# The opening of an attention and expert kernel: x in two halves, layer norm on DVE, high weights on ACT, first jobs round four banks, V among the maxima

## The reference

```
x = x + ln(attention(ln(x)))     16 heads of width 16; q, k, v, out projections with bias; softmax over 1024 keys
x = x + ln(experts(ln(x)))       16 gated experts of hidden width 128, top 8 by sigmoid gate, plus one shared expert
```

## Time and profile before

| | us |
|---|---|
| median of 3 runs | 2800.32 (2798.92 to 2801.91) |
| the profiled execution | 2801.8 |
| its span, first to last instruction | 2799.9 |
| PE busy, DVE busy | 2667.4 (95%), 2203.5 (79%) |
| first instruction on x (DVE statistics) | 6.37 |
| first maxima tile on PE | 45.36 |
| first score tile on PE | 93.11 |

### The profile page before, as it was taken

The page is one execution under the profiler, slowest core; times in us unless marked ns, Lnnn a source line. Parts: engine busy times, 40 slices in busy tenths (PEclk is TensorE's granted clock), DMA queues, the critical chain, the costliest instruction groups (busy, mean ns, idle before and its releaser), DMA issues.

```text
span 2799.9 us, 49038 instructions
## 1 busy us (share of the span) xinstructions
PE 2667.4 (95%) x17634; PEld 1756.9 (63%) x17634; DVE 2203.5 (79%) x4585; ACT 1628.2 (58%) x3159; POOL 1042.5 (37%) x1057
## 2 busy tenths in 40 slices
PE   5999999999999999999998999999999999999997
PEld 3445444454454444544543488888888888888886
DVE  5798999999999999999999576666666666666654
ACT  1578878878878888788788733333333333333332
POOL 4042563644635626545457453111111111111112
PEclk8899999999999999999999999999999999999999
DMA  5102223223123232320232323223232232222222
GB/s 119 27 28 58 66 72 71 61 66 66 43 66 66 61 71 59 79 66 28 66 80 88 90 69 103 76 72 81 84 84 80 72 82 83 79 71 84 80 72 53
DMA packets 126595, 197.39 MB, mean 70 GB/s; under 512 B 12288, under 2 KB 74768, under 8 KB 124304
## 3 DMA queue, kind: packets, MB, share of 16 engines
q1 hardware_dynamic: 126352, 194.25, 26.7%
HBM read 108.74 MB, written 17.30 MB: 45 GB/s over the span
## 4 chain that ended last, share of the span: by engine, by line
PE 72%; DVE 23%; issue 2%; POOL 1%; ACT 1%; DMA 0%; POOLq 0%; SPq 0%; ACTq 0%; DVEq 0%
DVE score_max L1122 18%; PE y_bank L746 14%; PE g_bank L732 13%; PE u_bank L732 13%; PE o_bank L572 12%; PE sm_bank L562 9%; PE st_bank L549 6%; PE job_bank L664 2%; DVE qk_parts L1144 1%; DVE xT_lo L1140 1%; PE job_bank L687 1%; PE job_bank L700 0%; DVE row_max L1129 0%; POOL x_in L1494 0%; DVE stats L1081 0%
## 5 line engine op out<-in xcount | busy, mean ns | idle before, releaser
L1122 DVE TENSOR_REDUCE score_max<-sm_bank 128x1 f32<-128x512 f32 x2048 | 1278.7, 683 | 96.1 <-PE sm_bank L562 92.1
L1014 ACT ACTIVATE probs<-st_bank 128x512 f32<-128x512 f32 x2023 | 1077.3, 604 | 273.4 <-PE st_bank L549 264.2
L562 PE MATMUL sm_bank<-qk_stack 64*128 64x512 f32 x2048 | 814.7, 459 | 78.6 <-DVE score_max L1122 72.1
L549 PE MATMUL st_bank<-qk_stack 64*128 64x512 f32 x2023 | 744.5, 426 | 1.8 <-ACT probs L1014 1.5
L562 PEld LDWEIGHTS sm_bank<-qk_stack 64*128 64x128 f32 x2048 | 363.0, 187 | 443.4 <-DVE score_max L1122 416.4
L572 PE MATMUL o_bank<-probs,v_quad 128*32 128x512 f32 x4096 | 549.4, 609 | 0.7 <-ACT probs L1014 0.7
L549 PEld LDWEIGHTS st_bank<-qk_stack 64*128 64x128 f32 x2023 | 350.1, 185 | 230.5 <-ACT probs L1014 189.4
L1269 DVE TENSOR_TENSOR h<-gate_act,u_bank 128x512 f32<-128x512 f32 x256 | 176.3, 689 | 311.4 <-ACT gate_act L968 311.3
L968 ACT ACTIVATE gate_act<-g_bank 128x512 f32<-128x512 f32 x272 | 163.0, 599 | 417.2 <-PE u_bank L732 417.1
L979 ACT ACTIVATE h_hi<-h 128x512 fp32r<-128x512 f32 x272 | 172.5, 634 | 325.3 <-DVE h L1272 287.8
L1552 POOL TENSOR_SCALAR f_x_in<-f_x_in,f_mv,f_rstd 128x256 f32<-128x256 f32 x64 | 90.5, 1424 | 616.9 <-DVE f_rstd L1183 616.9
(11 more groups left out here) (216 smaller groups left out, 4354.4 us busy)
## 6 DMA issues: line engine op xcount, KB each, us to landing
cb<-comb_dram SPq DMA_DIRECT2D x256, 256.0 KB, 3.4
qk_stack<-qk_parts SPq DMA_DIRECT2D x180, 256.0 KB, 5.5
x_in<-in_x SPq DMA_DIRECT2D x8, 1024.0 KB, 5.4
o_part<-o_sb SPq DMA_DIRECT2D x64, 128.0 KB, 2.7
sum_part<-o_sb SPq DMA_DIRECT2D x64, 128.0 KB, 2.8
x_res<-in_x SPq DMA_DIRECT2D x16, 512.0 KB, 3.9
x<-x_res SPq DMA_DIRECT2D x16, 512.0 KB, 3.6
f_x_in<-x SPq DMA_DIRECT2D x16, 512.0 KB, 3.9
```

Of the source, the lines that this page charges most:

```text
L549: mm(bank_of(tile)[:, :], k_stack[q][p][rows, kc * CH:(kc + 1) * CH], q_stack[q][p][rows, f * HALF:(f + 1) * HALF], start=True, stop=True) ...
L562: mm(sm_bank[n % RING][:, :], q_stack[q][p][rows, tok:tok + CH], k_stack[q][p][rows, half * HALF:(half + 1) * HALF], start=True, stop=True ...
L1014: nc.scalar.activation(probs[kc % 2][:, HEAD_AT[j], :], bank_of(4 * U + j)[:, :], ACT.Exp).then_inc(exp_done, 1)
L1122: v.reduce_max(score_max[f][:, HC * (2 * p + e) + c, half:half + 1], sm_bank[n % RING][:, :], AX_X).then_inc(smax_read, 1)
```

## The change

Six edits, all in the opening:

- x of batch 0 is loaded in two halves, each with a semaphore of its own (`half_loaded`). `ident`, the biases and `out_bias` are issued on ACT's queue; the raw weights have a semaphore each.
- The layer norm of batch 0 is wholly on DVE: statistics by half, aggregates, twelve steps of the reciprocal square root (`first_rstd`), eight normalisations. POOL's order becomes: memsets of quads 0 and 1, low parts of wv and wo, memsets of quads 2 and 3.
- ACT makes the four high parts as the weights arrive (with the 1/4 for q in it); DVE makes the low parts of wq and wk after the norm, POOL those of wv and wo. ACT waits for all low parts before QK job 4.
- The first jobs go round four banks (`job_bank`, `o_bank`, `st_bank` 0 and 1).
- On SP the first loads of the stacks leave out the small copy (a semaphore increment stands for it), and `load_x(1)` with `load_shift(0, 0)` comes after all four stacks.
- The V jobs are issued in pairs of matmuls, one pair behind each of the last 24 maxima tiles of step 1 (`first_v`).

```diff
-        first_bank = [job_bank, o_bank]
+        first_bank = [job_bank, o_bank, st_bank[0], st_bank[1]]
...
         def _(sp):
-            sp.dma_start(x_in[:, :, :], xv[:, 0:CHUNKS, :]).then_inc(x_loaded, 16)
-            sp.dma_start(ident[:, :], ident_dram).then_inc(const_loaded, 16)
+            for i in range(2):
+                half = slice(i * HC, (i + 1) * HC)
+                sp.dma_start(x_in[:, half, :], xv[:, half, :]).then_inc(half_loaded[i], 16)
             for n, w in (("q", wq), ("k", wk), ("v", wv), ("o", wo)):
-                sp.dma_start(w_raw[n], w.rearrange("(k p) d -> p k d", p=128)).then_inc(const_loaded, 16)
-            sp.dma_start(bias_raw[:, :, :], biases).then_inc(const_loaded, 16)
-            for i in range(2):
-                sp.dma_start(out_bias[:, i, :], ob.partition_broadcast(128)).then_inc(const_loaded, 16)
+                sp.dma_start(w_raw[n], w.rearrange("(k p) d -> p k d", p=128)).then_inc(w_raw_loaded[n], 16)
...
                     sp.wait_ge(st_ready, 4 * (UNITS * (B - 1) + 16 * (q + 1)))
-
-                sp.dma_start(qk_stack[q][SHIFT_ROW:SHIFT_ROW + 65:64, :, 0, :].bitcast(F32),
-                             qk_stack[q][ZERO_ROW:ZERO_ROW + 65:64, :, 0, :].bitcast(F32)).then_inc(stack_loaded[q][0], 16)
+                if first:
+
+                    sp.sem_inc(stack_loaded[q][0], 16)
+                else:
+
+                    sp.dma_start(qk_stack[q][SHIFT_ROW:SHIFT_ROW + 65:64, :, 0, :].bitcast(F32),
+                                 qk_stack[q][ZERO_ROW:ZERO_ROW + 65:64, :, 0, :].bitcast(F32)).then_inc(stack_loaded[q][0], 16)
                 for p in range(2):
...
             for q in range(QUADS):
-                if q == QUADS - 1:
-                    load_x(1)
-                    load_shift(0, 0)
                 sp.wait_ge(stacks_set, 5 * (q + 1))
                 load_stack(0, q, True)
+            load_x(1)
+            load_shift(0, 0)
...
-            pe.wait_ge(const_loaded, 16 * 8)
+            pe.wait_ge(const_loaded, 16 * 3)
             for n, (kind, i) in enumerate(FIRST_JOBS):
                 if (kind, i) == ("QK", 0):
-                    pe.wait_ge(weights_split, 9)
-                job(kind, 0, i, job_bank=first_bank[n % 2], banks=2)
-            pe.wait_ge(job_read["QK"], nth("QK", 0, 7))
-            before.clear()
+                    pe.wait_ge(weights_hi, 2)
+                    pe.wait_ge(weights_lo["dve"], 2)
+                job(kind, 0, i, job_bank=first_bank[n % 4], banks=4)
+
+            def first_v(n):
+
+                i, t = n // 6, n % 6
+                if t == 0:
+                    if i == 0:
+                        pe.wait_ge(job_read["XT"], nth("XT", 0, 3))
+                        pe.wait_ge(weights_hi, 4)
+                        pe.wait_ge(weights_lo["pool"], 2)
+                    pe.wait_ge(*before.pop(0))
+                    before.append((job_read["V"], nth("V", 0, i)))
+                steps = [(k, a, w) for k in range(KD) for a, w in PARTS]
+                c, bank = 2 * i + t // 3, first_bank[(i + 1) % 4]
+                for z in (2 * (t % 3), 2 * (t % 3) + 1):
+                    k, a, w = steps[z]
+                    last = mm(bank[:, (c % 2) * D:(c % 2 + 1) * D], xT[a][:, k, c * CH:(c + 1) * CH],
+                              w_parts["v"][w][:, k, :], start=(z == 0), stop=(z == len(steps) - 1))
+                if t == 5:
+                    last.then_inc(job_ready["V"], 1)
+
             for S in range(2):
...
                     smax(S, S, n // 4, n % 4, False)
+                    if S == 1 and n >= CHUNKS:
+                        first_v(n - CHUNKS)
                 if S == 0:
-                    job("SH", 0, 0)
-            for i in range(4):
-                job("V", 0, i, job_bank=first_bank[(i + 1) % 2], banks=2)
-            before.pop(0)
+                    job("SH", 0, 0, job_bank=first_bank[0], banks=4)
+            pe.wait_ge(job_read["V"], nth("V", 0, 2))
+            del before[:-1]
             for tile in range(8):
...
-            act.wait_ge(weights_split, 9)
+            act.dma_start(ident[:, :], ident_dram).then_inc(const_loaded, 16)
+            act.dma_start(bias_raw[:, :, :], biases).then_inc(bias_loaded, 16)
+            for i in range(2):
+                act.dma_start(out_bias[:, i, :], ob.partition_broadcast(128)).then_inc(const_loaded, 16)
+            for n in "qkvo":
+                act.wait_ge(w_raw_loaded[n], 16)
+                nc.scalar.activation(w_parts[n][0][:, :, :], w_raw[n], ACT.Copy,
+                                     scale=DH ** -0.5 if n == "q" else 1.0).then_inc(weights_hi, 1)
             act.wait_ge(bias_set, 2)
             for n, (kind, i) in enumerate(FIRST_JOBS):
-                job(kind, 0, i, first_bank[n % 2])
+                if (kind, i) == ("QK", 4):
+
+                    act.wait_ge(weights_lo["dve"], 2)
+                    act.wait_ge(weights_lo["pool"], 2)
+                job(kind, 0, i, first_bank[n % 4])
             job("SH", 0, 0)
             for i in range(4):
-                job("V", 0, i, first_bank[(i + 1) % 2])
+                job("V", 0, i, first_bank[(i + 1) % 4])
...
+            def first_rstd():
+
+                dve.wait_ge(mean_x_ready, CHUNKS)
+                v.tensor_scalar(var_x[:, :], mv_x[:, :, 1], EPS, None, ALU.add).then_inc(first_chain, 1)
+                dve.wait_ge(first_chain, 1)
+                v.tensor_scalar(rstd_x[:, :].bitcast(I32), var_x[:, :].bitcast(I32), 1, None,
+                                ALU.logical_shift_right).then_inc(first_chain, 1)
+                dve.wait_ge(first_chain, 2)
+                v.tensor_scalar(rstd_x[:, :].bitcast(I32), rstd_x[:, :].bitcast(I32), -1, RSQRT_SEED, ALU.mult,
+                                ALU.add).then_inc(first_chain, 1)
+                for i in range(3):
+                    dve.wait_ge(first_chain, 3 * i + 3)
+                    v.scalar_tensor_tensor(newton[:, :], rstd_x[:, :], -0.5, rstd_x[:, :], ALU.mult, ALU.mult).then_inc(first_chain, 1)
+                    dve.wait_ge(first_chain, 3 * i + 4)
+                    v.tensor_tensor(newton[:, :], newton[:, :], var_x[:, :], ALU.mult).then_inc(first_chain, 1)
+                    dve.wait_ge(first_chain, 3 * i + 5)
+                    v.scalar_tensor_tensor(rstd_x[:, :], newton[:, :], 1.5, rstd_x[:, :], ALU.add, ALU.mult).then_inc(first_chain, 1)
+                dve.wait_ge(first_chain, 12)
+
+            def first_weight_lo(n, scale):
+                dve.wait_ge(weights_hi, "qkvo".index(n) + 1)
+                v.scalar_tensor_tensor(w_parts[n][1][:, :, :], w_raw[n], scale, w_parts[n][0][:, :, :].bitcast(F32),
+                                       ALU.mult, ALU.subtract).then_inc(weights_lo["dve"], 1)
+
             for c in range(CHUNKS):
-                ln_x_stats(0, c)
+                if c % HC == 0:
+                    dve.wait_ge(half_loaded[c // HC], 16)
+                v.bn_stats(stats[:, c, :], x_in[:, c, :]).then_inc(stats_x_done, 1)
             for c in range(CHUNKS):
                 ln_x_aggr(0, c)
-            seed_x(0)
-            dve.wait_ge(const_loaded, 16 * 8)
-            v.tensor_scalar(scaled[:, :, :], w_raw["q"], DH ** -0.5, None, ALU.mult).then_inc(weights_split, 1)
+            first_rstd()
+            for c in range(CHUNKS):
+                v.tensor_scalar(x_in[:, c, :], x_in[:, c, :], mv_x[:, c, 0:1], rstd_x[:, c:c + 1],
+                                ALU.subtract, ALU.mult).then_inc(x_normed, 1)
+            dve.wait_ge(bias_loaded, 16)
             v.tensor_scalar(bias[:, 0, :], bias_raw[:, 0, :], DH ** -0.5, None, ALU.mult).then_inc(bias_set, 1)
             v.tensor_copy(bias[:, 1:3, :], bias_raw[:, 1:3, :]).then_inc(bias_set, 1)
+            first_weight_lo("q", DH ** -0.5)
+            first_weight_lo("k", 1.0)
             dve.wait_ge(bias_set, 2)
-            dve.wait_ge(weights_split, 1)
-            raw = {"q": scaled[:, :, :], "k": w_raw["k"], "v": w_raw["v"], "o": w_raw["o"]}
-            for n in "qkvo":
-                v.tensor_copy(w_parts[n][0][:, :, :], raw[n]).then_inc(weights_split, 1)
-            for i, n in enumerate("qkvo"):
-                dve.wait_ge(weights_split, 2 + i)
-                v.tensor_tensor(w_parts[n][1][:, :, :], raw[n], w_parts[n][0][:, :, :].bitcast(F32),
-                                ALU.subtract).then_inc(weights_split, 1)
-
             for n, (kind, i) in enumerate(FIRST_JOBS):
-                job(kind, 0, i, first_bank[n % 2])
+                job(kind, 0, i, first_bank[n % 4])
             for S in range(2):
...
             wait_apart(pool, two_set, 1, passed["pool"])
-            set_stacks(0)
-            norm_x(0)
-            for q in range(1, QUADS):
+            def first_weight_lo(n):
+                wait_apart(pool, weights_hi, "qkvo".index(n) + 1, passed["pool"])
+                g.tensor_tensor(w_parts[n][1][:, :, :], w_raw[n], w_parts[n][0][:, :, :].bitcast(F32),
```

(22 more changed lines are left out.)

## The result

The changed kernel takes 2811.45 us (median of 7, 2808.45 to 2813.82) against 2800.32 for the kernel before (7, 2796.5 to 2801.91): ratio 1.0038, 95% interval 1.0029 to 1.0047. I had forecast 2780, faster. Its profiled execution took 2809.14, with a span of 2807.3, 7.4 above the span before.

The account below looks back on a forecast made before the run. The prediction took the opening's chain of waits before the first score (93.11 us) as what the edits shorten, the PE/DVE-bound loop staying unchanged. Gains of 13.2 and 7.0 make 20.2 us off 2800.3, forecast 2780; range 2775 to 2787.

Parts of the forecast that it names:

- term 2: From the first maximum to the first score, now 47.75 us: 8.3 saved by dropping the V burst, less 1.3, gains 7.0.
- 0.43 + 2 x 0.21 = 0.85 a slot: Step 1: PE time at 1.2 GHz for one maximum and two V matmuls of 256 columns, against DVE's 0.595 us.
- rival 1: Step 1: V among the maxima doesn't lift the clock; 24 slots lag 5.8 us instead of 1.3, 2784.5; chance 0.14.
- the rise of the clock after 5.5 us of dense PE: Step 1: V among the maxima makes PE dense, so the clock rises after 5.5 us; lag until then 1.3 us.
- term 1: The start of the first maximum moves from 45.36 to 32.2 us: gains 13.2, with ends of 8 and 16.
- normalising on DVE ... I take 0.27: Layer norm of batch 0: each of eight 128x256 normalisations takes 0.27 us on DVE, all ready at 13.1.
- Rival 2: Opening norm: DVE waits behind POOL's two low parts, two waits of 1.29 make 2.6 us, 2782.6; chance 0.13.
- QK jobs 0 to 3: Opening: from the first QK matmul to the end of DVE's fourth, 9.73 us becomes 9.4 with four banks.
- SP to the first maximum: Stack 0: from SP's release to the first maximum, 7.45 us minus 0.73 for the copy of zeros is 6.7.
- A rise as early as 15.9 is the other end, 2.2 better: QK jobs in the opening: PE's clock may rise already at the first QK matmul, 15.9, making it 2.2 us better.
- My slower rival: Loop behind the first score: it stays at 1.2 GHz, each unit costs 1.09 us, about 2805 if 23 units; chance 0.02.
- signs of being wrong: First maximum after 36, the 0.85 spacing in step 1 lasting to the end, or loop units beyond the third differing in period.

Follow-up runs that it names:

- experiment 1: The changed kernel with the V jobs taken out from among the maxima and run as one burst behind them: 2799.36 us (median of 11).
- experiment 2: The changed kernel with V among reordered maxima, each V matmul cut into two of 64 rows, three halves behind each of 32 maxima: 2788.0 us, ratio to before 0.9963.
- experiment 5: The changed kernel with the same 48 V matmuls of 128 rows, but six in a row behind every fourth maximum of step 1: 2801.29 us.
- experiment 4: The changed kernel with V in row halves among the maxima and POOL quiet during DVE's norm: 2781.09 us, ratio to before 0.9933.
- experiment 3: The changed kernel with V as one burst behind the maxima and POOL kept quiet during DVE's layer norm: 2783.61 us, ratio to before 0.9953.
- experiment 7: Experiment 2 with another order on POOL, only memsets beside DVE's norm, the two low parts after them: 2787.1 us, measured one time.
- experiment 6: Experiment 2 with only the low parts of wv and wo beside DVE's norm, memsets of quads 1 to 3 waiting: 2783.54 us, measured one time.

## Why the prediction was wrong

**Wrong, term 2, "0.43 + 2 x 0.21 = 0.85 a slot".** This step decided the sign. I priced the V pair by its columns, measured in a burst of its own kind, and left out the change between matmuls of 64 and of 128 rows. It is 0.29 us, twice a slot: 1.45 measured. That is 24 slots 0.85 over DVE's 0.595, 20.4 us, of which the dropped burst gives back 8.3; 11.95 remain. Of the 0.85, 0.26 are columns at 1.2 GHz (6.2 us in all, my rival 1's price) and 0.59 the two changes (14.2 us in all). Experiments 1, 2 and 5 show it: without the pairs 12.9 us of the way to the first score are gone; in row halves a maximum follows V at its columns; and with a third of the changes 8.0 of the 12.9 are gone. The row was on hand and I read past it: the earlier trace rows has a maximum's weight load at 83.98 and the burst began at 84.7, 0.72 later, as after a change; I booked it as a hand-over. The loop itself cuts its jobs into row halves.

**Wrong, term 2, the rise of the clock after 5.5 us of dense PE.** It stayed at 0.50 throughout. My rival 1 named that outcome but priced it with the same 0.85, at 2784.5. In experiments 2 and 4, with no stall at row changes, the clock did rise, 7 and 13 us into the step.

**Wrong in size, term 1, "normalising on DVE ... I take 0.27".** The instruction by itself is 0.33 (experiments 3 and 4). Beside POOL the eight took 8.12 in the profiled execution, 5.9 over my 2.2; the norm began 1.2 late, with the two seed steps, and from its end to the first QK matmul it was 3.11 for 2.8. Term 1 is 5.9 instead of 13.2, below my lower end of 8. Rival 2 had the mechanism, with two waits of 1.29. The error was to count as partners only the two low parts: ten memsets stand right behind them on POOL, and experiment 7 shows that memsets block as well. The Trainium skill (SBUF — State Buffer, Who interferes with whom) says of a DVE instruction in a 2-port mode and any GpSimd instruction that the one that issues second blocks in full. Experiments 1, 6 and 7 agree, with DVE as the loser (no row shows in which mode the norm ran), and experiment 1 goes beyond a wait for one instruction: 10.28 us, for a row of eleven. For a DVE instruction with two SBUF inputs the same section of the Trainium skill has the blocking only beside a POOL instruction that reads SBUF, a limit that the prediction left out; the Newton steps beside memsets in experiment 7, at 0.17, agree.

**Right.** The chunks' statistics end near 7.8 (7.87). QK jobs 0 to 3 take 9.35 from the first matmul to DVE's fourth (9.4). SP to the first maximum takes 6.7 (32.71 to 39.44), without the zero copy. The move of `load_x(1)` and the added waits show no cost: the loop behind the first score is unchanged within 1.4. "A rise as early as 15.9 is the other end, 2.2 better" is what experiments 3 and 4 show (13.97 and 14.25 from the first QK matmul to the first maximum, where I had 16.3). Experiment 4, with both faults repaired, takes 2781.09, close to the 2780 that I had forecast for the changed kernel, but partly by luck: term 1 is 14.8 there, term 2 5.6.

**Range and rivals.** The range of 2775 to 2787 held neither this price nor its sign. My slower rival (the loop stays at 1.2 GHz) did not happen: the second unit period is 2.79. The clock that stays low and DVE's waits for POOL were among the rivals, the waits at 2.6 us where the norm lost 5.9; the change of row count, the largest term, was in none. Two of my signs of being wrong did come: the first maximum after 36, and a slot above 0.6 that lasts to the end (1.45, not even 0.85).

**What stays open.** The profiled executions of before and after are 7.4 apart, the medians 11.1. The norm of this code took 8.1, 13.5, 7.4 and 10.7 us in four traces (after, experiments 1, 2 and 5), so the waits of DVE for POOL fall differently each time. Behind the first score the traces differ too, from 2702.8 (experiment 7) to 2710.6 (experiment 3), in code that is the same. Which of the two makes the medians' rest was not shown. What keeps the clock at 0.50 in the changed kernel's step was not taken apart from the stalls: no run has them at a higher clock. Why one instruction of experiment 1 lost to eleven in a row, while others alternated with POOL one by one, was not found.

## What to carry to other kernels

Price a matmul that is moved between others by its neighbours and not by its own burst: where the row count changes between 64 and 128 from one to the next, PE paid about 0.29 us at 1.2 GHz, and a PE at 100% busy in the page doesn't show it. A DVE instruction such as this normalisation (one tensor as source, in SBUF, and the result in SBUF) needed POOL quiet for its whole length, memsets included; some 8 us of quiet on POOL made the first maximum 7.6 us earlier (experiment 4 against 2). When a change does six things and is slower, take it apart before it is dropped: with two of the six repaired it gave 0.67%. Of the other four only the four banks were tested alone.

## What the hardware showed that I had not expected

- A change between 64-row and 128-row matmuls costs 0.29 to 0.30 us at 1.2 GHz in both directions (0.72 and 0.73 where the columns are 0.43); between 64-row matmuls there was no such cost (0.21 from a V half to a maximum on the same rows).
- One DVE instruction of 0.33 us lasted 10.28 beside back-to-back POOL instructions, most of them memsets that read nothing. Newton steps with two tensors as source kept their 0.17 beside memsets.
- Behind four transposition jobs without a pause (12.43 to 16.1) QK matmuls had the distance of 2.4 GHz from the second on; with pauses of 1.2 us between the jobs and 0.8 us behind them it came 6.1 us after the first QK matmul.
